# Attention scores from two float32r parts on two halves of the partitions, in place of three bf16 parts

## What is computed

```python
q = _proj(query, wq, bq)
k = _proj(key, wk, bk)
v = _proj(value, wv, bv)
scores = jnp.einsum('bhqd,bhkd->bhqk', q, k) / jnp.sqrt(jnp.float32(DK))
scores = jnp.where(mask[:, None, :, :] == 0, -jnp.inf, scores)   # layer 0 only
p_attn = jax.nn.softmax(scores, axis=-1)
x = jnp.einsum('bhqk,bhkd->bhqd', p_attn, v)
```

## Time and profile before

| | us |
|---|---|
| median of three runs | 2009.93 |
| their range | 2009.01 to 2010.29 |
| span of the profiled execution | 1994.2 |
| layer 0: context, queries, attention | 0 to 444.4 |
| layer 0: output, experts | 444.4 to 992.8 |
| layer 1: queries, attention | 992.8 to 1690.0 |
| layer 1: output, experts | 1690.0 to 1994.2 |

### The profile page before, as it was taken

How to read it: one execution, slowest core, us unless ns; L and a number is a source line. 1 busy time by engine, 2 the same in 40 slices (tenths; PEclk the granted TensorE clock), 3 DMA queues, 4 the chain that set the end, 5 groups by cost and what they waited for, 6 DMA issues and landing times. The chain is left out here.

```text
span 1994.2 us, 26938 instructions
## 1 busy us (share of the span) xinstructions
PE 1696.5 (85%) x7786; PEld 785.9 (39%) x7809; DVE 1137.8 (57%) x2598; ACT 733.0 (37%) x942; POOL 178.3 (9%) x244
## 2 busy tenths in 40 slices
PE   6465999986999799999259999999999999795880
PEld 3131333326655466666212333333333332643550
DVE  5975778846211022222669888888888881531334
ACT  2022555551111121121013666666666667121110
POOL 3520000000120000000310000000000000042106
PEclk9685999997899899999666999999999999797995
DMA  6833211103000398886151110001000100234114
GB/s 215 268 103 108 58 32 30 31 11 107 11 32 1 115 328 288 309 299 229 48 165 58 34 29 16 16 15 28 15 15 15 29 0 1 73 98 140 39 43 131
DMA packets 112372, 178.64 MB, mean 90 GB/s; under 512 B 13775, under 2 KB 85659, under 8 KB 112283
## 3 DMA queue, kind: packets, MB, share of 16 engines
q1 hardware_dynamic: 105405, 162.87, 25.1%
q0 software_dynamic: 4608, 12.59, 2.0%
q10 hardware_dynamic: 2270, 2.17, 0.4%
HBM read 138.06 MB, written 39.13 MB: 89 GB/s over the span
## 5 line engine op out<-in xcount | busy, mean ns | idle before, releaser
L870 ACT ACTIVATE attend_probs<-attend_s_bank 128x1024 f32<-128x1024 f32 (+1 forms) x544 | 535.5, 1021 | 371.4 <-PE attend_s_bank L805 248.1
L887 DVE TENSOR_REDUCE attend_piece_max<-attend_p_bank 128x1 f32<-128x400 f32 (+1 forms) x1024 | 513.8, 564 | 90.7 <-PE attend_p_bank L794 80.6
L794 PE MATMUL attend_p_bank<-attend_k_st,attend_q_st 96*128 96x400 bf16 (+2 forms) x1280 | 401.2, 364 | 41.9 <-DMA attend_q_st<-q_parts 31.5
L805 PE MATMUL attend_s_bank<-attend_q_st,attend_k_st 99*128 99x512 bf16 (+1 forms) x1088 | 348.0, 383 | 3.6 <-DMA attend_q_st<-attend_m_part 1.4
L820 PE MATMUL attend_o_bank<-attend_probs,attend_v_st 128*32 128x512 f32 (+1 forms) x2176 | 291.5, 608 | 0.6 <-ACT attend_probs L870 0.6
L794 PEld LDWEIGHTS attend_p_bank<-attend_k_st,attend_q_st 96*128 96x128 bf16 x1280 | 109.5, 98 | 445.5 <-DVE attend_piece_max L887 295.7
L883 DVE CUSTOM_DVE_ANT_0 attend_junk<-attend_p_bank,window_mask_q 128x512 bf16<-128x512 f32 x256 | 168.7, 689 | 60.3 <-PE attend_p_bank L794 58.1
L805 PEld LDWEIGHTS attend_s_bank<-attend_q_st,attend_k_st 99*128 99x128 bf16 (+1 forms) x1088 | 105.8, 100 | 82.3 <-ACT attend_probs L870 21.0
L1497 DVE TENSOR_TENSOR slots_hid<-slots_b_bank,slots_g_act 128x512 f32<-128x512 f32 x46 | 31.8, 691 | 160.5 <-PE slots_b_bank L1391 160.5
L1278 DVE TENSOR_TENSOR share_hid<-share_b_bank,share_g_act 128x512 f32<-128x512 f32 (+1 forms) x40 | 27.6, 690 | 149.9 <-PE share_b_bank L1159 149.8
L1391 PE MATMUL slots_a_bank<-slots_w_up,slots_x_t 128*128 128x512 f32 x184 | 88.3, 603 | 6.8 <-DMA slots_w_up<-in_L_ffn_W_dram 6.8
(11 more groups left out here) (213 smaller groups left out, 1606.3 us busy)
## 6 DMA issues: line engine op xcount, KB each, us to landing
slots_w_up<-in_L_ffn_W_dram SPq DMA_DIRECT2D x46, 1024.0 KB, 7.0
slots_w_dn<-in_L_ffn_W_dram SPq DMA_DIRECT2D x23, 1024.0 KB, 7.4
ctx_raw<-in_mask_BxSxS_ik_dram SPq DMA_DIRECT2D x16, 800.5 KB, 6.1
attend_q_st<-q_parts SPq DMA_DIRECT2D x192, 64.0 KB
q_parts<-q_part SPq DMA_DIRECT2D x24, 256.0 KB, 2.0
sorted<-keep_zeros SPq DMA_DIRECT2D x6, 1024.0 KB, 7.7
back<-slots_y SPq DMA_DIRECT2D x13, 384.0 KB, 2.5
k_parts<-ctx_k_part SPq DMA_DIRECT2D x12, 400.2 KB, 3.0
```

The lines of the kernel that those rows point to most:

```text
L794: last = pe.matmul(bank[:, 0:kn], q_st[0:ROWS, slot, t * P:(t + 1) * P], k_st[0:ROWS, slot, k0:k0 + kn], start=True, stop=True)
L805: last = pe.matmul(out, k_st[:, hs, kt * P:kt * P + kn], q_st[:, hs, q0:q0 + CH], start=True, stop=not masked)
L870: act.activation(probs[0:kn, (kt + hs) % RING, half * HALF:(half + 1) * HALF], s_bank[half][0:kn, :], ACT.Exp).then_inc(exp_done, 1)
L887: dve.tensor_reduce(dst, bank_of(i, n)[:, 0:kn], AX.X, ALU.max).then_inc(entry_done, 1)
```

## The change

q and k are split into two parts each, rounded to float32r (a float32 of which TensorE uses a shortened mantissa); three products are kept, so the stack has 48 rows, 50 with the two parts of the maximum. ScalarE writes the high part itself in a second pass over the projection, and VectorE makes the low part by one subtraction. K and its ones stand on partitions 0 to 49 and again on 64 to 113; queries 0 to 1023 stand on the lower half, 1024 to 2047 on the upper. One half of the scores now is 512 queries from each side. Pieces take the two sides in turn. The ones come from DRAM by six DMAs on ScalarE's queue, stored there in the first block. The order of a step changes too: unmasked, one more entry stands ahead of the product with V; masked, two entries stand ahead of the scores and two between scores and product. Pieces are 402, 400, 400 and 399 keys (the last taken as 400). The branch for a mask without window, which these inputs don't take, drops its own masks.

```diff
-PART = 3
-ROWS = 6 * DK
+PART = 2
+ROWS = 3 * DK
 AUG = ROWS + PART
-PIECES = [(0, 401), (401, 400), (801, 400), (1201, 400)]
+SIDE = P // 2
+PIECES = [(0, 402), (402, 400), (802, 400), (1202, 399)]
...
+            sp.wait_ge(filled, 4)
+            sp.dma_start(scratch["ones"].rearrange("r (a q) -> (r a) q", q=P), const["ones"][0:PART * (KT + 1), :])\
+                .then_inc(ones_stored, 16)
+            sp.wait_ge(ones_stored, 16)
...
-                act.activation(k_full[:, b, k0:k0 + kn], bank[n % 2][:, 0:kn], ACT.Identity,
-                               bias=const["bqk"][:, (2 * l + 1) * DB + b:(2 * l + 1) * DB + b + 1]).then_inc(k_copied, 1)
+                for dst in (k_full[:, b], k_part[:, 0, b].bitcast(F32R)):
+                    act.activation(dst[:, k0:k0 + kn], bank[n % 2][:, 0:kn], ACT.Identity,
...
-                split_parts(dve, k_full[:, b], k_rest[:, :], [k_part[:, part, b] for part in range(PART)], split, 5 * n)
+                dve.tensor_tensor(k_part[:, 1, b].bitcast(F32R), k_full[:, b], k_part[:, 0, b], ALU.subtract)\
+                    .then_inc(split, 1)
...
-                split_parts(dve, full[:, b, at], rest[:, b, at], [part[:, k, b, at] for k in range(PART)], split, 5 * n)
+                dve.tensor_tensor(part[:, 1, b, at].bitcast(F32R), full[:, b, at], part[:, 0, b, at], ALU.subtract)\
+                    .then_inc(split, 1)
...
-        k_st = sc.sb("k_st", [AUG, RING, S], BF16)
-        q_st = sc.sb("q_st", [AUG, RING, T], BF16)
+        k_st = sc.sb("k_st", [P, RING, SP], F32)
+        q_st = sc.sb("q_st", [P, RING, HALF], F32)
...
-                for g, n in GROUPS_K:
-                    sp.dma_start(k_st[g * DK:(g + n) * DK, slot], scratch["k"][l, 0:n, ch, keys.slice(0, S)]).then_inc(stack_in[slot], 16)
-                for g, n in GROUPS_Q:
-                    sp.dma_start(q_st[g * DK:(g + 1) * DK, slot], scratch["q"][n, ch, :]).then_inc(stack_in[slot], 16)
+                for a in range(2):
+                    at = a * SIDE
+                    sp.dma_start(q_st[at:at + ROWS, slot], scratch["q"][:, ch, a * HALF:(a + 1) * HALF])\
+                        .then_inc(stack_in[slot], 16)
+                    for g, n in ((0, 2), (2, 1)):
+                        sp.dma_start(k_st[at + g * DK:at + (g + n) * DK, slot, 0:S],
+                                     scratch["k"][l, 0:n, ch, keys.slice(0, S)]).then_inc(stack_in[slot], 16)
...
-                    last = pe.matmul(bank[:, 0:kn], q_st[0:ROWS, slot, t * P:(t + 1) * P],
-                                     k_st[0:ROWS, slot, k0:k0 + kn], start=True, stop=True)
+                    a, t = divmod(t, QT // 2)
+                    rows = slice(a * SIDE, a * SIDE + ROWS)
+                    last = pe.matmul(bank[:, 0:even(kn)], q_st[rows, slot, t * P:(t + 1) * P].bitcast(F32R),
+                                     k_st[rows, slot, k0:k0 + even(kn)].bitcast(F32R), start=True, stop=True)
...
+            def products(hs, kt, half, start, stop):
+                kn = keys_of(kt)
+                for a in range(2):
+                    rows = slice(a * SIDE, a * SIDE + AUG)
+                    last = pe.matmul(s_bank[half][0:kn, a * CH:(a + 1) * CH],
+                                     k_st[rows, hs, kt * P:kt * P + kn].bitcast(F32R),
+                                     q_st[rows, hs, half * CH:(half + 1) * CH].bitcast(F32R), start=start, stop=stop)
+                return last
...
-                    wait(pe, exp_done, h * (2 * KT) + (2 * kt + half - 1))
+                    wait(pe, exp_done, h * (2 * KT) + (2 * kt + half - 1), apart=True)
...
+                if not masked:
+                    last = products(hs, kt, half, True, True)
+                elif half == 0:
+                    products(hs, kt, half, True, False)
+                    last = masks(kt, half, False, True)
+                else:
+                    masks(kt, half, True, False)
+                    last = products(hs, kt, half, False, True)
...
+                    if masked:
+                        for what, n in listed[s][0:2]:
+                            entry(i, slot, what, n)
...
-                    for what, n in listed[s][0:2]:
-                        entry(i, slot, what, n)
+                    if not masked:
+                        for what, n in listed[s][0:2]:
+                            entry(i, slot, what, n)
...
-                    for what, n in listed[s][2:3]:
+                    for what, n in listed[s][2:4]:
...
-                    for what, n in listed[s][3:]:
+                    for what, n in listed[s][4:]:
...
-                dve.tensor_scalar(m_part[:, prev, 0], turned, -1.0, None, ALU.mult).then_inc(max_split, 1)
...
+                dve.tensor_scalar(m_part[:, prev, 0].bitcast(F32R), turned, -1.0, None, ALU.mult).then_inc(max_high, 1)
+                wait(dve, max_high, i)
+                dve.scalar_tensor_tensor(out=m_part[:, prev, 1].bitcast(F32R), in0=turned, scalar=-1.0,
+                                         in1=m_part[:, prev, 0], op0=ALU.mult, op1=ALU.subtract).then_inc(entry_done, 1)
```

More of the change, by code:

```diff
@@ L23 @@
 F32 = mybir.dt.float32
+F32R = mybir.dt.float32r
 BF16 = mybir.dt.bfloat16
@@ L457, in _ @@
             for t in range(QT):
-                if not whole:
-                    pe.wait_ge(cut, t + 1)
+                pe.wait_ge(cut, t + 1)
                 if t >= 2:
@@ L538, in project_queries @@
         full = sc.sb("full", [P, DB, T], F32)
-        rest = sc.sb("rest", [P, DB, T], F32)
-        part = sc.sb("part", [P, PART, DB, T], BF16)
+        part = sc.sb("part", [P, PART, DB, T], F32)
         bias = sc.sb("bias", [P, DB], F32)
@@ L681, in entries_before, with number_of, tile_of @@
             return i * ENTRIES - 3 if not isinstance(i, int) or i <= H else H * ENTRIES - 1
+        def number_of(entry, *heads):
+            return next(n for step in entries(*heads)[0] for what, n in step if what == entry)
+        def tile_of(what):
+            pair, side = divmod(what, 2)
+            t, c = divmod(pair, NP)
+            return side * (QT // 2) + t, c
         def ring_of(i, n):
```

149 lines of the change are left out of this document (73 added, 76 removed).

## The result

The changed kernel takes 2153.3 us (median of 4 runs, 2130.0 to 2179.4) against 2009.5 before: ratio 1.068, 95% interval 1.062 to 1.075. Ratios, and e10's time, leave out the runs that lie more than 1.5% above the fastest of their kernel: 2179.4 here, one of e9 and two of e10, the profiled one among them. I had forecast 1897, in a range up to 1972, so not even the sign is right. The profiled execution has a span of 2145.9 against 1994.2, 151.7 more.

The account below looks back on a forecast made before the run. TensorE was taken as full in layer 0 and nearly full in layer 1, VectorE close behind and most used in context. Terms sum to -113: span 1994.2 to 1881, plus 15.7 gives 1897 us, range 1860 to 1930, up to 1972 with (a).

Parts of the forecast that it names:

- Float32r at one column per cycle, pairs abreast: Scores and pieces in both attentions: one pass per column, matmuls on different row halves run together, a 512-column pair costing 0.22.
- (a): Rival for scores and pieces: one pass, but row halves don't overlap; 1953 us, chance 0.17.
- (b): Rival at every score and piece matmul: 4-byte columns stream at half rate; about 2025 us, chance 0.14 with its worse form.
- Hidden, and were it late in layer 0, 0.5 us a head: Loading the next head's stack by six DMAs instead of nine: hidden, or at worst 0.5 us a head in layer 0.
- Granted clock: TensorE's clock, 0.98 in layer 1: its fall was named only as a sign of being wrong, the product with V taking 2.0.
- Layer 1, step of 2.60, -57 us: Layer 1 attention: paired scores and the new order shorten a step from 2.89 to 2.60, 195 steps, -57 us.
- my walk through the banks: Layer 1 step: a fourth piece ahead of the product with V cuts VectorE's wait from 0.39 to 0.13, step 2.54.
- A 4-byte weight load is 40 ns longer: Layer 1 step: the longer load falls into VectorE's wait once a step, part of going from 2.54 to 2.60.
- Rival (c): Weight loads bind: hidden by VectorE in layer 1, a pair waits perhaps 0.1 in layer 0, 26 us; 1923, no separate chance.
- Layer 0, head of 13.6, -29 us: Layer 0 attention: 16 fewer matmuls a head, less mode changes and loads; 15.4 to 13.6, -1.8 over 16 heads, -29 us.
- Context, -18: Context stage: one VectorE subtraction replaces five instructions a block, masks and DMA hold some back; -18 us of -24.
- Queries -7, last head -3, ones +1: Smaller terms: two query projections -3.5 us each, layer 1's last head's scores -3, storing the ones +1.

Follow-up runs that it names:

- e10: e9 with each score product of layer 1 issued twice into the same bank; 2059.3 us, ratio 1.024.
- e9: e1 with layer 1's product with V cut by columns, 256 of 512 queries, a piece, then the rest; 2211.8 us, ratio 1.0995.
- e1: Changed kernel with each head's stack loaded by twelve DMAs of 16 rows instead of six of 48, 32 and 16; 2065.6 us, ratio 1.030.
- e3: e1 with each score product of layer 1 issued twice into the same bank; 2013.3 us, ratio 1.0015.
- e18: e16 with no product issued twice; 2035.8 us, ratio 1.013.
- e16: e1 with layer 1's old order, the joined wait for the exponentials, and the first score product of a step issued twice; 1997.0 us, ratio 0.994.
- e14: Kernel before with half of layer 1's score columns left out, except for each head's first 128 keys; 1986.0 us, ratio 0.989.
- e17: e14 with fewer rows under layer 1's products, 48 of 96 for pieces and 35 of 99 for scores; 2138.3 us, ratio 1.069.
- e2: Kernel before with only the new order in layer 1, one more piece ahead of the product with V; 2016.4 us, ratio 1.0034.
- e4: e1 with the old order in layer 1, one piece fewer ahead of the product with V; 2029.7 us, ratio 1.0116.
- e5: e1 with layer 1's product with V issued in two halves by blocks, a piece between them; 2156.5 us, ratio 1.081.
- e8: Kernel before with layer 1's product with V issued in two halves by blocks, a piece between them; 2182.5 us, ratio 1.092.

## Why the prediction was wrong

- **Float32r at one column per cycle, pairs abreast: right.** Rivals (a) and (b) fall on the pair at 1193.08 and on 0.39 for 512 columns. But "fully abreast a pair costs 0.22" holds only behind a pair of the same kind: in e9 the score pair behind the product with V takes 0.33 to the start of the next pair, and the pieces behind that 0.19.
- **"Hidden, and were it late in layer 0, 0.5 us a head": wrong, the costliest step.** I priced the stack by its bytes and the number of issues; with up to 48 rows in one DMA it landed 7 us after its last issue, and a head stood 2.6 us on average, not 0.5. With the clock that fell along with these pauses it cost 84 us over 15 heads, which e1 took back by the shape alone.
- **Granted clock: not in the sum.** I named its fall only as what would make me wrong, and gave it no chance. In layer 1 it costs e1 52 us beside e3 and e18 39 beside e16. I had in mind a TensorE that is less busy because its columns go, and e14, which leaves as many out, keeps 0.98. Fewer rows and the overlap that they allow bring it down without float32r (e17), and every product of the change was to have half its rows.
- **Layer 1, step of 2.60, -57 us: wrong.** Measured 2.97 at full clock. (1) The pairs save 1.8 us of a head's busy time and not 5.6, and the step isn't the sum of TensorE's columns: e14 leaves as many columns out in the kernel before and gains 1.4 us a head, -20 us in all. (2) The order: my walk through the banks let a piece issue at the moment that VectorE begins a bank's successor (0.14 later in truth), the product with V 0.2 behind it (0.38) and VectorE 0.38 behind the product (0.485). With the measured ones the round trip of a bank is 0.14 + 0.38 + 1.00 + 0.485 and two more pieces of 0.48, 2.97, the step as it is. Moving the product costs 0.4 a head in the kernel before (e2) and 0.8 in the changed one (e4). (3) "A 4-byte weight load is 40 ns longer": 183 to 187 ns against 98, 85 longer. I took the price from a transpose (L789, 140) and let VectorE's wait hide it, but pieces that wait for a bank expose it every time: +3.0 us a head. The profile before had a nearer row, a 4-byte load of 128 columns that is no transpose:

```profile
L1413 PEld LDWEIGHTS slots_y_bank<-slots_w_dn,slots_hid_t 128*128 128x128 f32 x368 | 69.8, 190 | 20.0 <-issue 11.7
```

  Rival (c) was right that loads bind and wrong about the place: it let VectorE hide them in layer 1, where they cost most. The Trainium skill, "TensorE: Matmul & The Clock Gate", section Weight-path perf modes, denies float32 weights the fast load; the trace agrees, with 183 against 98 ns.
- **Layer 0, head of 13.6, -29 us:** 14.4 where the stack is in time, -12. The terms of the sum were the right ones and the changes between half and full rows under-priced: in e1 a pair of pieces or scores behind a change reads 0.49 to 0.50 where one behind another reads 0.40, and takes 0.33 to the next start where I had 0.22. The Trainium skill, "TensorEngine Tiling (Array Packing)", section Key Properties, has a drain for each change of tiling mode; the trace agrees in so far as behind a mask matmul that starts at 325.64 the scores' load starts only at 325.95 (e1), while the masks follow each other at 0.22. The 0.10 in the reading is no price of the change by itself: a lone piece whose load isn't hidden reads 0.10 more with no change before it.
- **Context, -18:** measured -9.5. VectorE fell by 31.4, inside my 25 to 33. But the masks' DMAs were the next to be late, and ScalarE, with its double copies, came late once for TensorE:

```profile
DVE keep_a_mask_all L349 <- DMA ctx_raw<-in_mask_BxSxS_ik_dram: 21.9, 12, 10.5
...
PE ctx_bank L286 <- ACT ctx_k_part L339: 13.3, 2, 12.5
```

  VectorE's wait for mask data was 6.4. The DMA share, 0.69, is now 0.77; I had given it and GpSimd together 6 of the 24 us.
- **Queries -7, last head -3, ones +1:** measured -7.5 and -0.8; the ones were not told apart. But the first head of layer 1 waits 29.4 us for its stack where it waited 23.5, another place in which the wide DMAs show (20.6 in e1).

The rival of a slower kernel rested on the wrong mechanism: what decided were two things that I had named and not priced, the landing of the stack and the clock.

**Open:** why e9, whose pieces and scores are e1's, has a clock of 0.65 against 0.84. What makes the heads at the loop's end longer than the others was not separated beyond the wait: 5 to 9 us in the variants whose clock holds, 2.5 to 4 in the kernel before. And whether rows alone or the overlap that they allow pulls the clock down in e17 is open: a run with both products on the same half of the rows, where they can't run side by side, would tell.

## What to carry to other kernels

Read a step as a round trip (bank read, load, product, bank full) before you price it by columns; leave work out in the old kernel, as e14 does, to see what a cheaper product can give. A change that halves the rows under a matmul may lower TensorE's clock even if no instruction has more to do, so look at the granted clock of the stretch first, and try repeated work as a probe. When a load's shape changes, price its landing and not its bytes.

## What the runs showed that I had not expected

- The granted clock went from 0.98 to 0.62 when the same bf16 products had fewer rows and so ran side by side (e14, e17), and from 0.85 to 0.97 when one score product in two was repeated (e18, e16).
- The six DMAs of 16 to 48 rows took some 9 us for 590 KB from first to last packet, 3.3 packets at a time; in twelve DMAs of 16 rows the same bytes took 5.8 us, 6 at a time, and TensorE never waited after the first head (e1).
- Four 32-column blocks of the float32 product run side by side: two take 1.05 us as four do (e5, e8).
- A float32r weight load of 128 columns takes 183 ns against 98 in bf16; where it is hidden the piece reads 0.34 us as in bf16, behind a wait 0.44.
